# Two merged instructions in a hat step, and a newly derived order of steps, in a convolution and attention kernel

## The chip, the cores and the metric

One Trainium2 chip, one of its cores. The metric is the device time of one launch in microseconds (us); a kernel's time is the median of its runs. The engines are PE (TensorE), DVE (VectorE), ACT (ScalarE), POOL (GpSimd) and SP (SyncE, which here only issues DMAs).

## The reference

Eight images of 56 x 56 places with 128 channels, in float32. Layer 0 is a deformable convolution and an MLP; layer 1 is additive attention and a mixture of 64 experts. Cut to what matters here:

```
xp = x @ w_in + b_in
h  = gelu(bn(depthwise_conv3x3(x)))
offset, mask = h @ w_off + b_off, softmax(h @ w_msk + b_msk)      # 4 groups x 9 taps
y  = bilinear_sample(pad(xp), offset) weighted by mask, summed over the taps, @ w_out
x  = x + gamma1 * layer_norm(y)
x  = x + gamma2 * layer_norm(gelu(x @ w_fc1) @ w_fc2)
# attention over the 3136 tokens t of an image
e  = exp(w2 . tanh(f[i] + g[j] + b1)) for j < i;  t = t + (e @ t) / sum(e)
# experts: per expert the 8 tokens with the highest softmax (over tokens) logits
pooled = sum of 8 tokens by their probability;  out = gelu(pooled @ w1) @ w2
t = t + scatter(out * probability)
```

## The kernel before

**Tiling.** An image is cut into 49 tiles of 64 places (the halves of the 128 partitions hold two pairs of groups), 25 blocks of 128 tokens (the last has 64) and 7 bands of 8 rows. A step is named by what it does and its number: sample 29 works on tile 29, keys 14 on block 14, offsets 6 on band 6.

**The samples.** For a tile, POOL issues an indirect gather for each of up to 18 columns (2 groups x 9 taps, line 1380). It gathers only 16 or 17 of them: the last one or two columns, the "near" ones, are made by PE from a map of the image in SBUF. For two such columns, DVE makes rows of a hat function (step rows, lines 1575 to 1592: how far row and column lie from the sample, clipped and turned to 1 - distance, then spread over four spans of the width), PE turns them (hat), DVE copies them (hat, line 1596), PE multiplies them with the map (near, line 2068), and DVE weighs and sums (near, lines 1602 and 1607). DVE weighs the gathered corners (weigh, line 1620, six instructions) and sums a tile (sample, line 1629). The gathered tiles lie in four slots of pool_mem; tile t may be gathered once the sample of the tile that had its slot is done (tile 4 waits for sample 0, tile 5 for sample 1, tile 33 for sample 29). From tile FULL on, the last image gathers all 18 columns; FULL comes out of the plan and is 4.

**A block's chain.** Two tiles give a block: turn, mix (layer norm, line 1463), turn_mid, hidden (PE, then ACT's gelu), mlp_out, norm, turn_norm, keys (line 1673). Then ACT runs the tanh units of the block (line 1938), whose number and width grow with the block's number; PE sums them (score, line 2128); ACT takes the exp (line 1948); PE turns and multiplies (values), with DVE's copy (line 1697) between; finish, norm2, route and logits follow. conv, offsets (lines 1504 to 1540) and weights (lines 1542 to 1574) make the indices and weights of a band. The steps image_in, project_in, patches, offsets, hat, near, route, logits and those below share one bank of PSUM, side_ps.

**The late work.** Experts can only be chosen when all of an image's logits exist. In the last image's time, the routes of images 0 and 1, 2 and 3, 4 and 5, and 6 are taken: u_in (SP loads the scores, line 1248), u_max, u_match, u_differ (DVE, lines 1745, 1754, 1759), u_exp, u_mul and the pooling. Then come 16 e_hid and 16 e_out (line 1817) for the experts of these seven images, c_expert (line 1822) and 49 c_mix (lines 2240 and 1828), which add the results to the images. The last image's own experts (l_ steps, from l_max at line 1832 on) stand at the end: 16 loads of 2 MB, four of them ahead.

**What sets the order.** Each engine's instructions stand in a fixed order, written by a planner in the same file. `simulate` runs a list scheduler over the steps with what each needs (`needs`), how long it lasts (`LASTS`, `STRETCH`) and when it is due (`due_times` plus a shift by kind, `SHIFT`; for the last image also `LATE_SHIFT`, `ROUTE_AT`, `EXPERT_GAP`). From its result `first_order` writes image 0, `list_schedule` a period that a loop repeats for images 1 to 6 (two images a turn), beginning at sample 0, and `last_order` the last image with the late work. POOL's order is that of the tiles. The step rows in the period needs for each image 36 of its kind; the launch has 255.

```
    todo += [(images - 1, e, s) for e, s in late]
    return in_order(simulate(need, due_of, todo, [x for x in at if x[3] < 0], stretch={"pool": SAMPLES / (NEAR_AT + .5)}))
```

These two lines (788 and 789) end `last_order`. The functions that the change touches:

Of the kernel before, what the change touches and what calls it, by code (L numbers as in the profile page):

```python
# [7 lines left out]
ALU = mybir.AluOpType  # L8
# [14 lines left out]
SAMPLES = GROUPS // 2 * TAPS  # L23
# [18 lines left out]
NEAR_AT = SAMPLES - NEAR  # L42
# [75 lines left out]
ROUTE_AT = (1.395, 5.421, 6.615, 10.365)  # L118
EXPERT_GAP = 0.2662
# [112 lines left out]
def last_user(t):  # L232
# [20 lines left out]
STRETCH = {'pe': 1.0669, 'act': 1.0220, 'dve': 1.0077}  # L253
# [8 lines left out]
    "keys": 2.361, "mix": 0.781, "conv": 1.814, "image_in": 1.885, "logits": -2.464, "patches": -1.253,  # L262
    "norm2": 3.532, "finish": -0.688, "mask": 0.74, "turn_norm": 0.831, "turn_mid": 0.867, "project_in": -1.682,
    "exp": -2.031, "weigh": 1.456, "unit": -2.536, "offsets": 0.04, "norm": -0.292, "values": 0.03, "score": -0.34,
    "mlp_out": -0.92, "x_in": -0.928, "rows": 2.531, "near": -0.291, "hidden": 0.256, "turn": -1.756,
    "sample": 1.692, "weights": 0.726, "route": -0.475, "hat": 0.361,
# [12 lines left out]
FIRST = ("image_in", "project_in", "patches")  # L279

# [5 lines left out]
    ("dve", "rows"): 2.0, ("pe", "hat"): .9, ("dve", "hat"): .8, ("pe", "near"): 1.3, ("dve", "near"): 1.4,  # L286
# [208 lines left out]
def simulate(need, due, todo, earlier=(), early=(), stretch={}, release=None):  # L495
# [10 lines left out]
    now = 0.0  # L506
# [32 lines left out]
    while True:  # L539
        for e in ready:  # L540
# [26 lines left out]
        now, _, what, e, n, step = event  # L567
        if what == "release":
            add(n, e, step)
            continue  # L570
        if what == "free":
            busy[e] = any(x[2] == "free" and x[3] == e for x in events)
        elif (n, step) in early:
            if e == "dve":
                banks[bank_of[n, step]] = True
        elif step[0] in SIDE and e == SIDE_READER.get(step[0], "dve"):
            side_free = True
# [188 lines left out]
def last_order(schedule, images):  # L766
# [16 lines left out]
    return in_order(simulate(need, due_of, todo, [x for x in at if x[3] < 0], stretch={"pool": SAMPLES / (NEAR_AT + .5)}))  # L783
# [44 lines left out]
def network(nc, io, x2_d, xln2_d, logits_d, patches_d, chosen_d, expert_d, map_d, out, images):  # L828
    with ExitStack() as ctx:
        def sb(name, shape, dt=F32):  # L830
            return ctx.enter_context(nc.sbuf_tensor(name, shape, dt))
# [61 lines left out]
        off_row = sb("off_row", [P, 2, H])  # L893
        off_col = sb("off_col", [P, 2, WINDOW])
# [499 lines left out]
        def _(dve):  # L1394
# [75 lines left out]
            def task(n, odd, name):  # L1470
# [104 lines left out]
                elif what == "rows":  # L1575
# [836 lines left out]
```

How the kernel before makes its waits and increments, by code:

```python
            def task(n, odd, name):  # L1170
                what, i = (*name, 0)[:2]
                b = i % 2
                if what == "image_in":
                    sp.wait_ge(band_turned.sem, band_turned.free(n, i, 2))
                    sp.dma_start(x_band[:, b], io["x"][bass.ds(n * S + i * BAND, BAND), :]
                                 .rearrange("(q p) c -> p q c", p=112)).then_inc(x_band_in[b].sem, 16)
                elif what == "patches":
                    sp.wait_ge(patch_ready.sem, patch_ready.after(n, i))
                    if i < 2 and not (isinstance(n, int) and n == 0):
                        sp.wait_ge(sampled.sem, sampled.after(n - 1, -1))
                    if is_early(n):
                        sp.dma_start(patches_d[0][i * P:i * P + patch_rows(i), :],
                                     early_patch[:patch_rows(i), i % EARLY_BANKS].rearrange("p g c k -> p (g c k)"))\
                            .then_inc(early_out[i % EARLY_BANKS], 16)
                        return
                    sp.dma_start(patches_d[int(odd)][i * P:i * P + patch_rows(i), :],
                                 patch[:patch_rows(i), b].rearrange("p g c k -> p (g c k)")).then_inc(patches_out[b].sem, 16)
                elif what == "map_out":
                    sp.wait_ge(in_copied.sem, in_copied.after(n, NBAND - 1))
                    nc.sync.sem_inc(sp_step, 1)
                    sp.wait_ge(map_in.sem, map_in.after(n - 1, 0))
```

## Time and profile before

| | us |
|---|---|
| median of 3 runs (8794.79 to 8805.16) | 8801.63 |
| profiled execution | 8798.16 |
| its span, first to last instruction | 8796.3 |
| first gather begins | 72.06 |
| last gather ends | 8481.51 |
| busy: PE 6909.1, DVE 6651.2, ACT 6757.9, POOL 6354.8 | |

The granted TensorE clock was 0.918 of full speed on average. Busy time leaves out the drains between DVE's dependent instructions and the issue time between POOL's gathers, so the engines are fuller than their shares say. The last image's gathers begin at 7358.4 us; the loop's images take 1036 to 1046 us each.

### The profile page before, as it was taken

The page shows a single profiled execution, that of the slowest core. Times are in us where ns is not written, and L with a number is a line of the kernel's source. Part 1 is how long each engine was busy: PE and PEld are TensorE (multiplying, and loading weights), DVE is VectorE, ACT ScalarE, POOL GpSimd, SP SyncE. Part 2 cuts the span into 40 slices and gives each one's busy share as a digit, 9 for nine tenths or more (in the row PEclk, how much of TensorE's full clock was granted, in tenths as well). Part 3 has the DMA queues.
Part 4 walks back from the last instruction along what each step waited for, and adds up shares of the span by engine and source line. Part 5 has one row for each costly group of instructions (what it writes and reads, how often), then busy time and mean ns, then how long its engine had stood idle before and what let it go on. Part 6 is the DMA issues. An engine that isn't in the chain of part 4 may idle for free.

```text
span 8796.3 us, 163541 instructions
## 1 busy us (share of the span) xinstructions
PE 6909.1 (79%) x50045; PEld 3461.2 (39%) x50045; DVE 6651.2 (76%) x18037; ACT 6757.9 (77%) x8222; POOL 6354.8 (72%) x6550
## 2 busy tenths in 40 slices
PE   5678878788777888778887788878887787767787
PEld 2333433434333333334334343343433333434444
DVE  6778877888778877788777887788877887776553
ACT  1358977788877888788977888768887788878992
POOL 4777777777777777777777777777777777777740
PEclk8789989899999999999998999989999999988997
DMA  3222222222222222222222222222222223335545
GB/s 90 61 79 74 61 61 61 81 70 61 63 68 78 65 63 61 72 80 60 63 60 79 75 62 61 61 83 67 62 63 69 78 64 70 106 101 168 143 125 183
DMA packets 554156, 693.05 MB, mean 79 GB/s; under 512 B 254400, under 2 KB 368960, under 8 KB 551136
## 3 DMA queue, kind: packets, MB, share of 16 engines
q0 software_dynamic: 209472, 429.42, 18.7%
q1 hardware_dynamic: 343808, 252.97, 10.2%
q8 instruction: 426, 6.98, 0.3%
q14 instruction: 450, 3.69, 0.1%
HBM read 568.99 MB, written 112.84 MB: 78 GB/s over the span
## 4 chain that ended last, share of the span: by engine, by line
POOL 38%; DVE 20%; issue 18%; PE 8%; ACT 7%; DVEq 7%; DMA 2%; SPq 0%; POOLq 0%; ACTq 0%
POOL pool_mem L1380 38%; DVEq L1399 6%; ACT tanh L1938 6%; DVE pool_mem L1620 3%; PE side_ps L2068 2%; PE score_ps L2128 2%; DVE y L1629 2%; DVE pool_mem L1607 1%; DVE hat L1602 1%; DVE bst L1446 1%; DVE expoT L1697 1%; DVE near_one L1438 1%; DVE pool_mem L1501 1%; PE side_ps L2038 1%; DVE hat L1589 1%
## 5 line engine op out<-in xcount | busy, mean ns | idle before, releaser
L1938 ACT ACTIVATE tanh<-key_rep,query 128x896 f32<-128x896 f32 (+7 forms) x6400 | 5539.3, 951 | 1131.2 <-DVEq L1399 582.0
L1380 POOL DMA_INDIRECT pool_mem<-patches_odd,pool_mem x3306 | 3214.0, 972 | 1034.3 <-issue 1002.6
L1380 POOL DMA_INDIRECT pool_mem<-patches_even,pool_mem x3240 | 3140.6, 969 | 1092.2 <-issue 978.2
L2128 PE MATMUL score_ps<-tanh,score_w 128*32 128x512 f32 (+3 forms) x24320 | 2680.0, 549 | 383.5 <-ACT tanh L1938 378.4
L2128 PEld LDWEIGHTS score_ps<-tanh,score_w 128*32 128x32 f32 x24320 | 692.4, 113 | 1803.0 <-issue 1140.4
L1620 DVE TENSOR_TENSOR pool_mem<-pool_mem 128x384 f32<-128x384 f32 (+2 forms) x2352 | 1070.2, 524 | 217.1 <-DMA pool_mem<-patches_even,pool_mem 107.5
L2068 PE MATMUL side_ps<-near_map,hatT 112*64 112x480 f32 x4080 | 1051.3, 638 | 202.0 <-DVEq L1399 180.8
L1629 DVE TENSOR_REDUCE y<-pool_mem 128x64 f32<-128x2304 f32 x392 | 999.0, 2548 | 30.8 <-issue 9.9
L2157 PE MATMUL value_ps<-values,expoT 128*128 128x129 f32 (+1 forms) x5200 | 784.9, 292 | 59.4 <-DVE expoT L1697 54.0
L2157 PEld LDWEIGHTS value_ps<-values,expoT 128*128 128x128 f32 (+1 forms) x5200 | 685.4, 199 | 174.3 <-DVE expoT L1697 105.4
L1697 DVE COPY expoT<-turn_ps 128x512 f32<-128x512 f32 (+4 forms) x800 | 456.1, 571 | 172.7 <-issue 100.7
L2007 PE MATMUL turn_ps<-ident,expo 128*128 128x128 f32 (+1 forms) x2632 | 465.0, 292 | 112.9 <-DVE expoT L1697 49.8
L2068 PEld LDWEIGHTS side_ps<-near_map,hatT 112*64 112x64 f32 x4080 | 294.7, 148 | 654.0 <-issue 636.0
L1948 ACT ACTIVATE expo<-score_ps,tiny 128x896 f32<-128x896 f32 (+9 forms) x416 | 382.9, 920 | 156.8 <-PE score_ps L2128 151.2
L1602 DVE TENSOR_TENSOR hat<-side_ps,off_col 128x480 f32<-128x480 f32 x510 | 333.2, 653 | 164.2 <-PE side_ps L2068 137.7
L2007 PEld LDWEIGHTS turn_ps<-ident,expo 128*128 128x128 f32 (+1 forms) x2632 | 313.4, 149 | 314.9 <-issue 149.8
L2038 PE MATMUL side_ps<-pool_mem,early 128*128 128x448 f32 x1008 | 408.2, 560 | 32.9 <-DVEq L1399 32.8
L1607 DVE TENSOR_REDUCE pool_mem<-hat 128x32 f32<-128x480 f32 x510 | 333.8, 655 | 60.9 <-issue 1.4
L1948 ACT ACT_TABLE_LOAD x196 | 251.5, 1283 | 138.1 <-PE score_ps L2128 134.6
L1923 ACT ACTIVATE hid<-chain_ps,b_hid 128x128 f32<-128x128 f32 (+1 forms) x800 | 227.0, 366 | 111.2 <-PE chain_ps L2097 109.4
L2007 PE MATMUL side_ps<-ident,hat 128*112 128x128 f32 x1020 | 191.9, 304 | 151.1 <-DVEq L1399 142.6
L2104 PE MATMUL chain_ps<-w_fc,hid 128*128 128x128 f32 (+1 forms) x1600 | 236.9, 293 | 80.1 <-ACT hid L1923 79.5
(192 smaller groups left out, 7394.9 us busy)
## 6 DMA issues: line engine op xcount, KB each, us to landing
pool_mem<-in_weight SPq DMA_DIRECT2D x64, 1024.0 KB, 9.1
pool_mem<-patches_odd,pool_mem POOLq DMA_INDIRECT x3306
pool_mem<-patches_even,pool_mem POOLq DMA_INDIRECT x3240
patches_even<-pool_mem SPq DMA_DIRECT2D x104, 256.0 KB, 2.0
patches_odd<-pool_mem SPq DMA_DIRECT2D x104, 256.0 KB
pool_mem<-in_x SPq DMA_DIRECT2D x56, 224.0 KB
x_tok<-in_x SPq DMA_DIRECT2D x192, 64.0 KB
x_d<-x SPq DMA_DIRECT2D x192, 64.0 KB
```

What stands on the lines that cost most here:

```text
L1380: pool.indirect_dma_start(gathered[:, b, j * 4 * CG:(j + 1) * 4 * CG], None, patches_flat[int(odd)], bass.IndirectOffsetOnAxis(ap=index[:, ...
L1399: return v.drain()
L1620: v.tensor_tensor(part, part, weight[:, lo:hi].unsqueeze(2) .to_broadcast([P, hi - lo, CG, 4]), ALU.mult)
L1629: v.tensor_reduce(y[:, i // 2 % 2, b].rearrange("p (g c) -> p g c", c=CG), product.rearrange("p (g t) c k -> p g c t k", g=2), AX_XY, ALU. ...
L1697: last = v.tensor_copy(expoT[:rows_, pi % 2, z[0]:z[1], :r], turn_ps[:rows_, z[0]:z[1], :r])
L1938: nc.scalar.activation(tanh[:, TANH_AT[ui][0]:TANH_AT[ui][1]], key_rep[:, lo:lo + w], ACT.Tanh, bias=query[:, col:col + 1]).then_inc(tanh_ ...
L1948: nc.scalar.activation(expo[:r, ci % 2, :w], score_ps[:r, ci % 2, :w], ACT.Exp, bias=tiny[:r, 2:3])\
L2007: return mm(out, src, ident[:r, :r], is_transpose=True, start=True, stop=True)
L2038: last = mm(side_ps[:, :BAND], taps[:, t], x_pad[:, i * BAND_ROWS + dy:(i + 1) * BAND_ROWS + dy, dx:dx + W], start=t == 0, stop=t == TAPS - 1)
L2068: last = mm(side_ps[h * SUB:(h + 1) * SUB, :CG * WINDOW], hatT[:HALF_ROWS, b, part, h * SUB:(h + 1) * SUB], near_map[:HALF_ROWS, h, part], ...
L2128: last = mm(score_ps[32 * col:32 * col + 32, ci % 2, lo:hi], score_w[:, place], tanh[:, TANH_AT[ui][0] + lo:TANH_AT[ui][0] + hi], start=pl ...
L2157: last = mm(value_ps[:r, :C + 1], expoT[:wj, pi % 2, z, :r], values[:wj, value_place(odd, j)], start=j == 0, stop=j == k)
```

## The change

The rows and columns of the hat lie in one tile, `off`, of 56 + 15 values for each of two samples. The subtractions stay two instructions; the mirror (negative distance) and the clip are now one each over both. The step has five instructions, not seven. The planner is changed with it: rows lasts 1.75, not 2.0, the side bank is free for PE's next step as soon as DVE has read it in near and offsets (0.8 and 0.85 after the begin), the gather time of the last image is given tile by tile, and the numbers that shift the steps are others. FULL is 6, not 4, so that the last image's tiles 4 and 5 gather 17 and 16 columns and three near columns more are made; there are 257 rows steps.

```diff
-ROUTE_AT = (1.395, 5.421, 6.615, 10.365)
-EXPERT_GAP = 0.2662
+ROUTE_AT = (0.665, 1.92, 5.635, 7.017)
+EXPERT_GAP = 0.1326
...
-STRETCH = {'pe': 1.0669, 'act': 1.0220, 'dve': 1.0077}
+STRETCH = {'pe': 1.0560, 'act': 1.0116, 'dve': 0.9975}
...
-    "sample": 1.692, "weights": 0.726, "route": -0.475, "hat": 0.361,
+    "sample": 4.156, "score": -0.806, "turn": -1.86, "turn_mid": 0.602, "turn_norm": 0.831, "unit": -1.662,
...
+SIDE_READ = {"near": .8, "offsets": .85}
...
-    ("dve", "rows"): 2.0, ("pe", "hat"): .9, ("dve", "hat"): .8, ("pe", "near"): 1.3, ("dve", "near"): 1.4,
+    ("dve", "rows"): 1.75, ("pe", "hat"): .9, ("dve", "hat"): .8, ("pe", "near"): 1.3, ("dve", "near"): 1.4,
...
+        if step[0] in SIDE_READ and engine == "dve" and at + SIDE_READ[step[0]] > 0:
+            events.append((at + SIDE_READ[step[0]], serial, "side", engine, n, step))
+            serial += 1
...
+            if e == "pool" and whole is not None and n == whole[0] and step[1] >= whole[1]:
+                end = now + SAMPLES * GATHER_US
...
-        off_row = sb("off_row", [P, 2, H])
-        off_col = sb("off_col", [P, 2, WINDOW])
+        off = sb("off", [P, 2, H + WINDOW])
+        off_row, off_col = off[:, :, :H], off[:, :, H:]
...
-                    v.scalar_tensor_tensor(off_row[:, :m], off_row[:, :m], -1.0, off_row[:, :m], ALU.mult, ALU.min)
-                    v.scalar_tensor_tensor(off_col[:, :m], off_col[:, :m], -1.0, off_col[:, :m], ALU.mult, ALU.min)
-                    settle()
-                    v.tensor_scalar(off_row[:, :m], off_row[:, :m], -1.0, 1.0, ALU.max, ALU.add)
-                    v.tensor_scalar(off_col[:, :m], off_col[:, :m], -1.0, 1.0, ALU.max, ALU.add)
+                    v.scalar_tensor_tensor(off[:, :m], off[:, :m], -1.0, off[:, :m], ALU.mult, ALU.min)
+                    settle()
+                    v.tensor_scalar(off[:, :m], off[:, :m], -1.0, 1.0, ALU.max, ALU.add)
                     settle()
```

Three places show how the steps move. The changed file has up to nine lines more, so that L2068 becomes L2075, L2007 becomes L2014, L1629 becomes L1636.

**The end of the loop's period, PE.** Before, from turn 24 (chain_ps from y) to near 4 (side_ps from near_map), the last PE step of the period:

```order
L2080 MATMUL chain_ps<-ident,y 64x64 x4
L1983 REGISTER_ALU
L2128 MATMUL score_ps<-tanh,score_w 32x512 x4
L2128 MATMUL score_ps<-tanh,score_w 32x384 x4
L1983 REGISTER_ALU
L2128 MATMUL score_ps<-tanh,score_w 32x512 x4
L2128 MATMUL score_ps<-tanh,score_w 32x384 x4
L1983 REGISTER_ALU
L2007 MATMUL turn_ps<-ident,expo 128x128 x4
L1990 REGISTER_ALU
L2068 MATMUL side_ps<-near_map,hatT 64x480 x4
```

After, from turn_norm 23 over keys 23 and near 5 to turn 24 (near 4 stands just ahead of the piece):

```order
L2014 MATMUL chain_ps<-ident,values 128x128
L1990 REGISTER_ALU
L2135 MATMUL score_ps<-tanh,score_w 32x512 x4
L2135 MATMUL score_ps<-tanh,score_w 32x384 x4
L2120 MATMUL chain_ps<-chainT,w_key 128x128
L2121 MATMUL chain_ps<-chainT,w_q 128x128
L1997 REGISTER_ALU
L2075 MATMUL side_ps<-near_map,hatT 64x480 x4
L1990 REGISTER_ALU
L2014 MATMUL turn_ps<-ident,expo 128x128 x4
L1990 REGISTER_ALU
L2087 MATMUL chain_ps<-ident,y 64x64 x4
```

Near 4 and near 5 have moved from behind turn 24 to ahead of it. On DVE, mlp_out 23, norm 23 and offsets 6 have moved the other way past weigh 2, from behind it to ahead of it, and rows 3 stands ahead of sample 0.

**The last image's first route, DVE.** MAX is u_max 0, y is a sample. Before, samples 0 to 2 are done (the last two are shown) and weights 6, mlp_out 24 and norm 24 lie between them and MAX:

```order
L1629 TENSOR_REDUCE y<-pool_mem 128x64
L1648 COPY chainT<-chain_ps 128x64
L1629 TENSOR_REDUCE y<-pool_mem 128x64
...
L1660 TENSOR_SCALAR values<-x,mv,root 64x128
L1697 COPY expoT<-turn_ps 128x512
L1745 MAX early<-pool_mem 128x8
L1747 TENSOR_SCALAR early<-early 128x1
```

After:

```order
L1655 COPY chainT<-chain_ps 128x64
L1752 MAX early<-pool_mem 128x8
L1754 TENSOR_SCALAR early<-early 128x1
L1761 MATCH_REPLACE pool_mem<-early,pool_mem 128x3136
L1766 TENSOR_TENSOR pool_mem<-pool_mem 128x448 x7
L1472 TENSOR_TENSOR ln_a<-chain_ps,rows 64x128
...
L1627 TENSOR_TENSOR pool_mem<-pool_mem 128x128
L1673 COPY chainT<-chain_ps 128x64
L1704 COPY expoT<-turn_ps 128x512
L1636 TENSOR_REDUCE y<-pool_mem 128x64
```

The three steps of the route, then mlp_out 24, norm 24 and weigh 3, stand ahead of sample 0; weights 6, mix 24 and turn_mid 24 are what stands before MAX in the last image's part.

**The end, DVE.** L1828 is a c_mix, MAX is l_max, the row with x7 holds the seven l_turn. Before:

```order
L1733 TENSOR_SCALAR logit<-side_ps,gate_b 64x64
L1832 MAX early<-tanh 64x8
L1834 TENSOR_SCALAR early<-early 64x1
L1835 MATCH_REPLACE tanh<-early,tanh 64x3136
L1837 TENSOR_TENSOR tanh<-tanh 64x3136
L1828 TENSOR_TENSOR pool_mem<-pool_mem,side_ps 112x512 x2
L1841 RECIPROCAL early<-early 64x1
L1843 SCALAR_TENSOR_TENSOR tanh<-tanh,early 64x3136
L1828 TENSOR_TENSOR pool_mem<-pool_mem,side_ps 112x512
L1847 COPY tanh<-score_ps 112x256 x7
```

After:

```order
L1740 TENSOR_SCALAR logit<-side_ps,gate_b 64x64
L1839 MAX early<-tanh 64x8
L1841 TENSOR_SCALAR early<-early 64x1
L1842 MATCH_REPLACE tanh<-early,tanh 64x3136
L1844 TENSOR_TENSOR tanh<-tanh 64x3136
L1848 RECIPROCAL early<-early 64x1
L1850 SCALAR_TENSOR_TENSOR tanh<-tanh,early 64x3136
L1854 COPY tanh<-score_ps 112x256 x7
```

The c_mix are gone from this place: 39 of 49 stood ahead of l_max before, all 49 do now. Their first stands behind keys 14, not keys 17; e_hid begins behind keys 9, not 11, and e_out behind keys 12, not 14.

## Rows read from the trace of the kernel before

**Rows 1.** The page: the chain that ended last, and POOL's two groups.
```profile
POOL 38%; DVE 20%; issue 18%; PE 8%; ACT 7%; DVEq 7%; DMA 2%; SPq 0%; POOLq 0%; ACTq 0%
L1380 POOL DMA_INDIRECT pool_mem<-patches_odd,pool_mem x3306 | 3214.0, 972 | 1034.3 <-issue 1002.6
L1380 POOL DMA_INDIRECT pool_mem<-patches_even,pool_mem x3240 | 3140.6, 969 | 1092.2 <-issue 978.2
```

**Rows 2.** Waits, POOL, whole span: us in total, times, longest.
```profile
POOL pool_mem L1380 <- DVE y L1629: 74.1, 45, 13.7
```

**Rows 3.** Waits, POOL, from 1118 to 7358 us (images 1 to 6).
```profile
POOL pool_mem L1380 <- DVE y L1629: 55.9, 42, 8.3
```

**Rows 4.** Timeline, POOL: start us, us, [idle before]; image 0 tile 5, image 7 tile 4.
```profile
191.06 0.94 POOL L1380 DMA_INDIRECT pool_mem<-patches_even,pool_mem  x1 [13.68 <-DVE y L1629]
...
7446.07 0.94 POOL L1380 DMA_INDIRECT pool_mem<-patches_odd,pool_mem  x1 [4.23 <-DVE y L1629]
```

**Rows 5.** Window 8300:8600 (PE, PEld, DVE, ACT, POOL busy), and ACT's waits in 8582:8641.
```profile
8300.00:8600.00 300.00, 254.84 (x1854) 142.86 (x1850) 148.18 (x383) 294.02 (x320) 138.24 (x143) 0.95 0.41 118
...
ACT expo L1948 <- PE score_ps L2128: 6.7, 2, 6.4
```

**Rows 6.** Timeline, DVE: a near, a copy and a rows step in image 5.
```profile
5324.24 0.65 DVE L1602 TENSOR_TENSOR hat<-side_ps,off_col 128x480 f32<-128x480 f32 x1
...
5326.01 0.27 DVE L1578 TENSOR_TENSOR off_row<-near_y,ruler 128x112 f32<-128x112 f32 x1
...
5327.04 0.18 DVE L1587 TENSOR_SCALAR off_col<-off_col 128x30 f32<-128x30 f32 x1
...
5328.12 0.16 DVE L1707 TENSOR_SCALAR den<-value_ps 128x1 f32<-128x1 f32 x1 [0.21 <-issue]
```

**Rows 7.** Timeline, POOL: the gather over the end of that rows step.
```profile
5326.58 0.96 POOL L1380 DMA_INDIRECT pool_mem<-patches_odd,pool_mem  x1 [0.30 <-issue]
```

**Rows 8.** Timeline, DVE, image 7: weigh 2, mlp_out 23, turn_norm 23, offsets 6, turn 24, sample 0.
```profile
7423.22 2.80 DVE L1620 TENSOR_TENSOR pool_mem<-pool_mem 128x384 f32<-128x384 f32 x6 [8.02 <-DMA pool_mem<-patches_odd,pool_mem]
...
7426.99 0.29 DVE L1463 TENSOR_TENSOR ln_a<-chain_ps,rows 128x128 f32<-128x128 f32 x1
...
7434.79 0.29 DVE L1666 COPY chainT<-chain_ps 128x128 f32<-128x128 f32 x1 [0.48 <-PE chain_ps L2007]
...
7436.94 0.42 DVE L1509 TENSOR_TENSOR pool_mem<-side_ps,grid 128x252 f32<-128x252 f32 x1
...
7441.61 0.29 DVE L1635 COPY chainT<-chain_ps 128x128 f32<-128x128 f32 x1 [0.26 <-issue]
...
7442.75 2.54 DVE L1629 TENSOR_REDUCE y<-pool_mem 128x64 f32<-128x2304 f32 x1
```

**Rows 9.** Timelines, DVE and SP, image 7: weights 6, the route's first load, u_max, u_match, u_differ.
```profile
7458.97 0.28 DVE L1544 TENSOR_REDUCE pool_mem<-pool_mem 128x14 f32<-128x126 f32 x1
...
7462.76 0.39 SPq L1239 DMA_DIRECT2D early<-in_weight  x1
...
7475.79 3.43 DVE L1745 MAX8 early<-pool_mem 128x8 f32<-128x3136 f32 x1 [7.17 <-DMA pool_mem<-logits_d]
...
7480.08 3.41 DVE L1754 MATCH_REPLACE8 pool_mem<-early,pool_mem 128x3136 f32<-128x3136 f32 x1
...
7486.06 3.84 DVE L1759 TENSOR_TENSOR pool_mem<-pool_mem 128x448 f32<-128x448 f32 x7
```

**Rows 10.** The line of e_out (ns min/median/max, first and last start), and c_expert in the timeline.
```profile
L1817 DVE COPY pool_mem<-side_ps x16: 280/292/292, 8123.6 to 8230.1; 128x128 f32<-128x128 f32 x16
...
8238.39 1.23 DVE L1822 TENSOR_TENSOR pool_mem<-pool_mem,early 128x1024 f32<-128x1024 f32 x1 [6.76 <-DMA pool_mem<-expert_d]
```

**Rows 11.** c_mix from 8640 us on and DVE's waits for it; window 8697:8771 of the loads.
```profile
L1828 DVE TENSOR_TENSOR pool_mem<-pool_mem,side_ps x14: 672/688/689, 8641.0 to 8777.7; 112x512 f32<-112x512 f32 x14
...
  DVE pool_mem L1828: 17.8, 11
...
8697.00:8771.00 74.00, 46.65 (x588) 25.45 (x580) 16.07 (x41) 2.80 (x13) 0.00 (x0) 0.79 0.97 348
```

More of the change, by code:

```diff
@@ L261 @@
 LATE_SHIFT = {
[L262 to L265, printed above, removed]
-    "sample": 1.692, "weights": 0.726, "route": -0.475, "hat": 0.361,
+    "conv": 0.912, "exp": -2.106, "finish": -0.559, "hat": -0.168, "hidden": 0.967, "image_in": 1.885, "keys": 2.361,
+    "logits": -2.464, "map_in": 0.428, "mask": -0.934, "mix": 0.781, "mlp_out": -0.92, "near": 1.076, "norm": -0.246,
+    "norm2": 2.196, "offsets": -2.031, "patches": -0.849, "project_in": -1.682, "route": -0.475, "rows": 2.283,
+    "sample": 4.156, "score": -0.806, "turn": -1.86, "turn_mid": 0.602, "turn_norm": 0.831, "unit": -1.662,
+    "values": 2.049, "weigh": 1.456, "weights": 1.186, "x_in": -0.514,
 }
@@ L492, in needs, with simulate @@
     return out
-def simulate(need, due, todo, earlier=(), early=(), stretch={}, release=None):
+def simulate(need, due, todo, earlier=(), early=(), stretch={}, release=None, whole=None):
     waiting, users = {}, {}
@@ L567, in simulate @@
         now, _, what, e, n, step = event
+        if what == "side":
+            side_free = True
+            continue
         if what == "release":
@@ L575, in simulate @@
                 banks[bank_of[n, step]] = True
-        elif step[0] in SIDE and e == SIDE_READER.get(step[0], "dve"):
+        elif step[0] in SIDE and step[0] not in SIDE_READ and e == SIDE_READER.get(step[0], "dve"):
             side_free = True
@@ L782, in last_order @@
     todo += [(images - 1, e, s) for e, s in late]
-    return in_order(simulate(need, due_of, todo, [x for x in at if x[3] < 0], stretch={"pool": SAMPLES / (NEAR_AT + .5)}))
+    return in_order(simulate(need, due_of, todo, [x for x in at if x[3] < 0], whole=(images - 1, full)))
 def units_of(images):
```

## The prediction

> **What bounds the kernel now.** I read the page first, then the waits of POOL, then the timelines around them. The page says that POOL issues 3306 + 3240 = 6546 gathers of 0.97 us each, and that the chain of waits lies on POOL and on "issue" for 56% of the span, on DVE for 20% [rows 1]. The busy share (72%) hides that POOL is full: between two gathers lie 0.30 us of issue, so a gather costs about 1.275 us, and the only other idle time after the first one is 74.1 us in 45 waits for y, that is for the step sample to free a slot [rows 2]. Each of the 45 contains the ordinary 0.30 us, so 60.6 us are real. Of these the loop's six images hold 55.9 - 42 x 0.30 = 43.3 us [rows 3], image 0 holds 13.68 - 0.30 = 13.4 us at tile 5, and the last image 4.23 - 0.30 = 3.9 us at tile 4 [rows 4]. What follows the last gather (the table above has its end), some 315 us, is bound first by ACT, busy for 294.0 of 300 us before 8600 us [rows 5], and then by the expert loads. ACT is fed by the tiles: in the last image its tanh units wait for the keys of their block until block 17, and from then on it never runs dry. A shift of the gathers up to block 17 therefore moves the end by as much.
>
> **The step rows.** It loses two of seven instructions, 0.18 us each in the 1.90 us from 5326.01 to 5327.91 [rows 6]. Over the 257 steps that is at most 257 x 0.36 = 93 us of DVE time and likelier a third of that, since the two that stay read 142 columns instead of 112. None of it counts: POOL is not waiting for it, and DVE's own idle gaps before weigh (8.02 us in the place shown further down) take it up. If this cover were gone, 36 steps an image at 0.13 us would be 5 us an image. The gather that ran while L1587 did took 0.96 us beside its usual 0.94 [rows 7]; 0.02 us for each of 255 steps would be 5 us, and I count none. Beside that row stands a rule of the Trainium skill (SBUF — State Buffer, Who interferes with whom): a VectorE instruction that uses both ports locks GpSimd out of the shared pair until it ends, and then GpSimd can write no DMA descriptors. By that rule a removed TENSOR_SCALAR of this kind gives its whole length back to POOL; that is a rival below, since here the row shows a tenth of it.
>
> **The loop's order.** Before, sample 0 of the next image (which frees the slot of tile 4) stands behind weigh 2, hat 2, mlp_out 23, norm 23, offsets 6 and more: 19.5 us from the start of weigh 2, itself held by its gather, to the start of sample 0 [rows 8]. The new order has mlp_out 23, norm 23 and offsets 6 ahead of weigh 2, and puts near 4, near 5 and rows 3 behind it. What is left behind weigh 2: weigh 2 itself 2.80 + 0.14, turn_norm and keys 7436.94 - 7434.31 = 2.6, turn 24 and a copy 7442.75 - 7441.35 = 1.4 [rows 8], two nears at 1.6 and a rows at 1.8 [rows 6]; together 11.9 us. Sample 0 would begin at 7423.2 + 11.9 = 7435.1 and end at 7437.7; POOL comes to tile 4 at 7446.07 - 4.23 + 0.30 = 7442.1 [rows 4]. That leaves 4.4 us to spare where it lacked 4 to 8. The loop's other tight place is sample 29, which frees the slot of tile 33 (the rest of the 43.3 us). It stood behind weigh 31; now weigh 29 is the last ahead of it, two tiles or some 33 gathers (42 us) earlier. I take 43.3 us as gone but for 3 us of chance waits; bounds: all gone, or 15 us left.
>
> **The first image.** Sample 1 stood behind weigh 4, held by its gather. It now stands behind weigh 3, whose gather lands 17 x 1.275 = 21.7 us earlier: it ends near 191.06 - 21.7 = 169.4, and tile 5 is reached at 191.06 - 13.4 = 177.7 [rows 4]. The wait of 13.4 us goes; the way to the first gather is unchanged.
>
> **The last image.** Here the change adds a wait. The route of images 0 and 1 begins with loads that SP may issue only after weights 6; u_max began 7475.79 - 7462.76 = 13.0 us later and DVE stood 7.17 us for it, but behind sample 0 [rows 9]. The new order puts u_max, u_match and u_differ ahead of sample 0. From the end of the shortened stretch, at the image's start + 76 us, it goes: hat 3 and weights 6 (7462.76 - 7458.97 = 3.8) to 81, the loads to 94, u_max 3.6, u_match 3.6, u_differ 4.0 [rows 9], then mlp_out 24 and norm 24 (5 us: for block 23 the stretch from 7426.99 to 7434.31 holds them and four copies [rows 8]), weigh 3 at 2.9, sample 0 at 2.5 with copies around them: 117. POOL reaches tile 4 at 84. It waits 33 us instead of 3.9: 29.1 us given back. Queued behind are image 6's copies for PE and, through PE, ACT; both have room before block 17. Bounds: 10 us if the loads land early, 45 if PE is late too. Three gathers fewer (the full tiles start at 6, not 4) give 3 x 1.275 = 3.8 us.
>
> **The end.** The experts' steps come two to four blocks earlier. The 16 e_out took 106.5 us and c_expert stood 6.76 us for its load, just as ACT entered its full stretch [rows 10]; now they fall on blocks 12 to 14. There they delay keys 14 by up to 20 us, of which ACT can recover about 14 before block 17, and the stall at block 17 is gone; I take these as even, bounds -5 and +15. All 49 c_mix now stand before l_max; before, 14 of them ran after 8641 us, and DVE waited 17.8 us for them [rows 11]. Ten lie between ACT's last exp and the first new load, and with their 0.69 us each they held that chain by up to 18 us; I take 12, since some waits were covered by ACT and PE. During the loads DMA is at 0.97 with or without them [rows 11], so there only 4.5 us more. PE is relieved of 4 or 5 c_mix after keys 24, where ACT's last exp waited 6.4 us for it [rows 5]: 4 us. The end gives 20.5; bounds 0 and 33.
>
> **The sum:** -13.4 - 43.3 + 3 + 29.1 - 3.8 + 0 - 20.5 = -48.9 us. Against the profiled execution's 8798.16 us, which is 3.5 us under the median, this is 8749.3 us.
>
> **Rivals.**
> 1. *Slower: the loop's sample 0 comes late after all.* Near 4, near 5 and rows 3 now stand before it, each through the one side bank of PE, which has scores of its own between them. The mechanism costs six times its wait. It cancels the 48.9 at 8 us an image and makes the kernel slower by 0.2% at 11, so sample 0 would have to come 15.6 us later than I count. For it: DVE waits for L1602 occur. Against: in this place turn_norm waited only 0.48 us for PE [rows 8]. At 13 us an image: -48.9 - 3 + 78 = +26, 8824 us.
> 2. *The end gives nothing and keys 14 stays late.* The expert loads bound the end with or without c_mix, and the packed e_out cost 15 us at block 17: -48.9 + 20.5 + 15 = -13.4, 8785 us. For it: DMA at 0.97 in the loads. Against: ten c_mix lie ahead of them.
> 3. *The last image does not stall.* If the route's load is there when DVE comes, the 29.1 us stay: 8720 us. For it: DVE is often held elsewhere; against: 13.0 us of load follow weights 6 in any order.
> 4. *The port.* If every TENSOR_SCALAR removed gave its 0.18 us back to POOL, 255 x 0.18 = 46 us more: 8703 us. Against it, the 0.96 beside 0.94 us. This is the Trainium skill's lock, named above.
> 5. *The change does nothing where it counts:* the plan moves steps but DVE waits for the same gathers, and only the end differs: -13.4 - 3.8 - 4 = -21, 8777 us.
>
> **How the numbers follow.** My case 0.66, rival 5 0.05, rival 3 0.08, rival 4 0.02, rival 2 0.12, rival 1 0.07. The range 8720 to 8786 takes in rivals 2, 3 and 5; outside lie rivals 1 and 4 and the tails of my case, together under 0.2. Against the median 8801.63 a difference of 0.2% is 17.6 us, about what a measurement can tell from no change. My case and rivals 3, 4 and 5 are faster by more: 0.81. Rival 2 and my case's slow edge: 0.12. Slower by more than 0.2%: 0.07.
>
> **What would show it.** Right: POOL's waits for y fall from 74.1 us to some 35 to 45 and are nearly all one wait in the last image at tile 4; no wait at tile 5 of image 0; DVE stands about 9 us before the first MAX8, which comes ahead of the image's first y; no row of L1828 (c_mix) behind the last MAX8; ACT's last exp near 8607, the last gather near 8453. Wrong: waits of 3 us or more at tile 4 in the loop's images (rival 1), or MAX8 for image 7 following ACT's last exp as late as before, 14 us (rival 2).

## The result and the profile after

The changed kernel takes 8750.5 us (median of 3 runs, 8747.33 to 8752.43) against 8801.63: a ratio of 0.9943, 95% interval 0.9920 to 0.9965. The forecast was 8749.3. From one profiled execution to the other (8798.16 to 8752.43) the change is 45.7 us, where 48.9 were forecast.

The page of the changed kernel, its span, busy times, the chain that ended last and POOL's two groups, beside [rows 1]:

```profile
span 8750.6 us, 163133 instructions
...
PE 6894.0 (79%) x50077; PEld 3450.2 (39%) x50077; DVE 6621.8 (76%) x17545; ACT 6769.0 (77%) x8236; POOL 6352.6 (73%) x6547
...
POOL 50%; issue 19%; DVE 12%; ACT 7%; PE 6%; DVEq 4%; DMA 2%; SPq 1%; POOLq 0%; ACTq 0%
...
L1389 POOL DMA_INDIRECT pool_mem<-patches_odd,pool_mem x3303 | 3208.3, 971 | 1042.5 <-issue 1004.0
L1389 POOL DMA_INDIRECT pool_mem<-patches_even,pool_mem x3240 | 3144.1, 970 | 1058.6 <-issue 983.4
```

The gathers are as long as before, and DVE is busy for 29.4 us less, of which little or nothing was waited for in this kernel (e2, e8 below). What has gone is waiting: POOL and its issue are now 69% of the chain, before 56%, DVE 12%, before 20%. POOL's waits for y over the whole span (us in total, times, longest), then the same from 1103 to 7303 us, the loop's six images, which answer to [rows 2] and [rows 3]:

```profile
POOL pool_mem L1389 <- DVE y L1636: 42.2, 21, 36.1
...
POOL pool_mem L1389 <- DVE y L1636: 5.5, 18, 0.3
```

In the loop the longest is 0.3 us, the ordinary issue time: none of 42 waits is left. POOL's timeline at tile 5 of image 0 and at tile 4 of image 7, beside [rows 4] (start us, us, [idle before]):

```profile
178.91 0.94 POOL L1389 DMA_INDIRECT pool_mem<-patches_even,pool_mem  x1 [0.30 <-issue]
...
7422.66 0.94 POOL L1389 DMA_INDIRECT pool_mem<-patches_odd,pool_mem  x1 [36.07 <-DVE y L1636]
```

The first wait is gone; the second has grown from 4.23 to 36.07 us and is nearly all that is left of the 42.2. What holds it: the route's first load on SP (image 7 begins at 7302.7 us),

```profile
7384.88 0.42 SPq L1248 DMA_DIRECT2D early<-in_weight  x1
```

and then DVE's timeline, from the last copy ahead of u_max to weigh 3 and sample 0:

```profile
7388.38 0.23 DVE L1655 COPY chainT<-chain_ps 128x64 f32<-128x64 f32 x1
7399.38 3.43 DVE L1752 MAX8 early<-pool_mem 128x8 f32<-128x3136 f32 x1 [10.77 <-DMA pool_mem<-logits_d]
...
7415.84 2.62 DVE L1627 TENSOR_TENSOR pool_mem<-pool_mem 128x384 f32<-128x384 f32 x6
...
7419.33 2.54 DVE L1636 TENSOR_REDUCE y<-pool_mem 128x64 f32<-128x2304 f32 x1
```

The loads begin 82.2 us into the image, MAX8 (u_max) comes 14.5 us later, and sample 0 starts 116.6 us into the image. At the other end, ACT's last exp with its wait for PE, beside [rows 5]:

```profile
8605.41 0.95 ACT L1955 ACTIVATE expo<-score_ps,tiny 64x832 f32<-64x832 f32 x1 [3.58 <-PE score_ps L2135]
```

Then the lines of c_mix and of l_max with first and last start, beside [rows 11]; no c_mix is left behind l_max:

```profile
L1835 DVE TENSOR_TENSOR pool_mem<-pool_mem,side_ps x49: 674/686/690, 8078.4 to 8552.7; 112x512 f32<-112x512 f32 x49
...
L1839 DVE MAX8 early<-tanh x1: 3420/3420/3420, 8617.1 to 8617.1; 64x8 f32<-64x3136 f32 x1
```

The same marks in both kernels give a ledger that adds up to the two spans (us, each rounded by itself, so that a row can be off by 0.1; POOL's last gather ends, ACT's last exp begins, l_max begins, the span ends):

| | last gather | to last exp | to l_max | to the end | span |
|---|---|---|---|---|---|
| before | 8481.5 | 157.7 | 14.8 | 142.4 | 8796.3 |
| after | 8453.9 | 151.5 | 11.7 | 133.5 | 8750.6 |
| difference | -27.6 | -6.2 | -3.1 | -8.8 | -45.7 |

### The profile page after: what moved, and what is told of

The parts are those of the page before. It is cut to its first block, busy times and chain, and to the rows that moved or that the text cites. A ratio compares the mean times of both kernels' runs of the same rounds, so it can differ in the third digit from the quotient of the medians.

```text
span 8750.6 us, 163133 instructions
## 1 busy us (share of the span) xinstructions
PE 6894.0 (79%) x50077; PEld 3450.2 (39%) x50077; DVE 6621.8 (76%) x17545; ACT 6769.0 (77%) x8236; POOL 6352.6 (73%) x6547
## 3 DMA queue, kind: packets, MB, share of 16 engines
q1 hardware_dynamic: 343808, 252.97, 10.2%
## 4 chain that ended last, share of the span: by engine, by line
POOL 50%; issue 19%; DVE 12%; ACT 7%; PE 6%; DVEq 4%; DMA 2%; SPq 1%; POOLq 0%; ACTq 0%
POOL pool_mem L1389 50%; ACT tanh L1945 6%; DVEq L1408 3%; DVE pool_mem L1627 2%; DVE y L1636 2%; PE score_ps L2135 1%; PE side_ps L2075 1%; DVE pool_mem L1614 1%; PE value_ps L2164 1%; DVE hat L1609 1%; DMA expert_d<-pool_mem 0%; DVE hat L1596 0%; DMA pool_mem<-in_weight 0%; DVE bst L1455 0%; PE side_ps L2045 0%
## 5 line engine op out<-in xcount | busy, mean ns | idle before, releaser
L2075 PE MATMUL side_ps<-near_map,hatT 112*64 112x480 f32 x4104 | 1022.2, 620 | 209.8 <-DVEq L1408 208.1
L1636 DVE TENSOR_REDUCE y<-pool_mem 128x64 f32<-128x2304 f32 x392 | 997.8, 2547 | 20.8 <-issue 6.6
L2014 PE MATMUL turn_ps<-ident,expo 128*128 128x128 f32 (+1 forms) x2632 | 470.8, 293 | 101.6 <-DVE expoT L1704 38.0
L2075 PEld LDWEIGHTS side_ps<-near_map,hatT 112*64 112x64 f32 x4104 | 288.7, 144 | 663.6 <-issue 647.7
L2014 PEld LDWEIGHTS turn_ps<-ident,expo 128*128 128x128 f32 (+1 forms) x2632 | 316.5, 150 | 293.8 <-issue 168.3
L1609 DVE TENSOR_TENSOR hat<-side_ps,off 128x480 f32<-128x480 f32 x513 | 334.7, 652 | 120.3 <-PE side_ps L2075 96.2
L2014 PE MATMUL side_ps<-ident,hat 128*112 128x128 f32 x1028 | 203.6, 317 | 175.0 <-DVEq L1408 170.6
L2104 PE MATMUL chain_ps<-chainT,w_fc 128*128 128x128 f32 (+1 forms) x1600 | 247.6, 302 | 113.8 <-DVE chainT L1655 113.4
```

Source lines behind the costliest of these rows:

```text
L1609: v.tensor_tensor(part, side_ps[:, :CG * WINDOW].rearrange("p (c x) -> p c x", x=WINDOW), off_col[:, i % 2:i % 2 + 1, :].to_broadcast([P, ...
L1636: v.tensor_reduce(y[:, i // 2 % 2, b].rearrange("p (g c) -> p g c", c=CG), product.rearrange("p (g t) c k -> p g c t k", g=2), AX_XY, ALU. ...
L2014: return mm(out, src, ident[:r, :r], is_transpose=True, start=True, stop=True)
L2075: last = mm(side_ps[h * SUB:(h + 1) * SUB, :CG * WINDOW], hatT[:HALF_ROWS, b, part, h * SUB:(h + 1) * SUB], near_map[:HALF_ROWS, h, part], ...
```

## The experiments

The changed kernel was timed beside the kernel before on its own; the others were timed in four sessions (e1 to e4, e5 to e8, e9 to e11, e12) beside it, so the table gives ratios to before of the same session. The median of before was 8801.63 us in the first of these sessions and 8794.3 to 8798.47 in the four others, so medians of different sessions compare to within some 7 us only. The ledger's columns come from each kernel's profile.

| kernel | us (runs) | ratio, 95% interval | waits for y | last gather | to last exp | to l_max | to the end | span |
|---|---|---|---|---|---|---|---|---|
| after | 8750.5 (3) | 0.9943, 0.9920 to 0.9965 | 42.2 | 8453.9 | 151.5 | 11.7 | 133.5 | 8750.6 |
| e1 | 8788.83 (11) | 0.9991, 0.9982 to 1.0000 | 61.0 | 8469.4 | 160.3 | 14.8 | 145.2 | 8789.6 |
| e2 | 8755.51 (5) | 0.9951, 0.9937 to 0.9964 | 35.7 | 8456.5 | 153.1 | 12.0 | 133.3 | 8754.9 |
| e3 | 8723.73 (5) | 0.9916, 0.9902 to 0.9929 | 7.9 | 8418.0 | 161.0 | 11.6 | 136.9 | 8727.5 |
| e4 | 8784.34 (10) | 0.9993, 0.9977 to 1.0009 | 65.9 | 8482.5 | 149.2 | 11.7 | 133.9 | 8777.3 |
| e5 | 8738.19 (5) | 0.9936, 0.9922 to 0.9949 | 7.9 | 8415.2 | 158.3 | 15.8 | 142.4 | 8731.7 |
| e6 | 8763.99 (5) | 0.9964, 0.9951 to 0.9978 | 40.1 | 8442.0 | 151.9 | 17.5 | 142.4 | 8753.8 |
| e7 | 8757.85 (5) | 0.9960, 0.9946 to 0.9973 | 54.3 | 8458.9 | 151.3 | 11.7 | 133.9 | 8755.8 |
| e8 | 8747.36 (5) | 0.9946, 0.9933 to 0.9960 | 38.8 | 8446.8 | 153.3 | 11.6 | 134.2 | 8746.0 |
| e9 | 8738.85 (5) | 0.9937, 0.9924 to 0.9951 | 7.0 | 8418.7 | 172.5 | 11.2 | 135.8 | 8738.2 |
| e10 | 8727.60 (5) | 0.9925, 0.9912 to 0.9939 | 4.9 | 8414.7 | 156.9 | 19.8 | 135.5 | 8726.9 |
| e11 | 8810.39 (11) | 1.0021, 1.0012 to 1.0030 | 73.2 | 8479.8 | 178.5 | 15.3 | 134.4 | 8808.1 |
| e12 | 8728.87 (5) | 0.9920, 0.9907 to 0.9934 | 9.5 | 8417.3 | 159.4 | 15.4 | 135.3 | 8727.4 |

Waits for y of 5 to 8 us in total are the ordinary issue times alone.

### e1: the merged step alone

The kernel before with the five instructions and nothing of the planner.

```diff
-                    v.scalar_tensor_tensor(off_row[:, :m], off_row[:, :m], -1.0, off_row[:, :m], ALU.mult, ALU.min)
-                    v.scalar_tensor_tensor(off_col[:, :m], off_col[:, :m], -1.0, off_col[:, :m], ALU.mult, ALU.min)
+                    v.scalar_tensor_tensor(off[:, :m], off[:, :m], -1.0, off[:, :m], ALU.mult, ALU.min)
                     settle()
-                    v.tensor_scalar(off_row[:, :m], off_row[:, :m], -1.0, 1.0, ALU.max, ALU.add)
-                    v.tensor_scalar(off_col[:, :m], off_col[:, :m], -1.0, 1.0, ALU.max, ALU.add)
+                    v.tensor_scalar(off[:, :m], off[:, :m], -1.0, 1.0, ALU.max, ALU.add)
```

> The kernel before with the merged rows step alone (five instructions), the planner and so the order of steps as before. My theory (only the order counts, POOL is the path): 8800 us, within 5 us of before, with POOL's waits for y at 70 to 75 us in 45 times and DVE's busy time some 35 us less. Rival (the DVE time that the merge saves is what was gained): 8750 to 8770 us.

POOL's waits for y in it, beside [rows 2]:

```profile
POOL pool_mem L1380 <- DVE y L1627: 61.0, 40, 13.7
```

It gives 6.6 us (8788.83 against 8795.42), and the interval of its ratio reaches 1.0000, so this is at the edge of the noise. The waits shrink by 13.1 us, 11.3 us of it real waits in the loop (43.3 to 32.0); the 13.4 us in image 0 stay. I had expected them to stay at 70 to 75 us, and that was wrong. The last gather ends 12.1 us sooner and the span shrinks by 6.7, since the end is 5.4 us worse. So the step is worth something where samples are late: about a seventh of the 45.7 us, and far from the rival's 8750 to 8770 us.

### e2: the order alone

The changed kernel with the seven instructions (the diff of e1 the other way round).

> The changed kernel with the rows step's mirror and clip as four instructions again (seven in all), its order of steps kept. My theory: 8750 us, at most 5 us more, since DVE's 0.13 us a step does not reach POOL; POOL's only long wait stays the one of 33 to 37 us at tile 4 of the last image. Rival (the merge is the gain): 8780 to 8800 us.

It has no wait for y but the one of 33 us and lies 4.3 us above the changed kernel's span; the two ratios overlap. The new order carries the gain.

### e3: sample 0 ahead of the route

```diff
-    "sample": 4.156,
+    "sample": 2.5,
```

> The changed kernel with the last image's shift of sample at 2.5 instead of 4.156, so that sample 0 and samples 1 and 2 stand ahead of u_max 0. My theory (the last image's wait of 35.8 us at tile 4 is all given back at the end, since ACT from block 17 on follows POOL): the wait falls under 5 us and the time to 8719 us, between 8710 and 8730. Rival (the end is bound by ACT's total work or by PE, so the wait was hidden): 8745 to 8750 us.

POOL waits for y nowhere:

```profile
POOL pool_mem L1389 <- DVE y L1636: 7.9, 26, 0.3
```

The last gather comes 35.9 us sooner than in the changed kernel, the end 23.1 us sooner: 9.5 us are lost again on the way to the last exp and 3.4 behind it. At 8723.73 us this is the fastest of all. It was not timed beside the changed kernel: the intervals of the two ratios, 0.9902 to 0.9929 and 0.9920 to 0.9965, still touch, and it is the ledger that says where the 23.1 us come from.

### e4, e7 and e8: more and less DVE time in the step, and the port

e4 issues the mirror three times, e7 the clip three times (the first two with `+ 0.0`), e8 leaves the mirror out, so that its near columns are weighted otherwise.

```diff
+                    v.tensor_scalar(off[:, :m], off[:, :m], -1.0, 0.0, ALU.max, ALU.add)
+                    settle()
+                    v.tensor_scalar(off[:, :m], off[:, :m], -1.0, 0.0, ALU.max, ALU.add)
+                    settle()
                     v.tensor_scalar(off[:, :m], off[:, :m], -1.0, 1.0, ALU.max, ALU.add)
```

> The changed kernel with the mirror instruction issued three times (the second and third change nothing), order kept: 257 steps longer by two instructions of about 0.31 us and their drains, some 0.78 us each, 200 us of DVE time. My theory: DVE's slack takes nearly all of it; one rows step stands between weigh 2 and sample 0, so sample 0 comes 0.8 us later and has 4 to spare: 8750 to 8760 us. Rival (DVE is as full as POOL): over 8850 us.

> The changed kernel with the clip (TENSOR_SCALAR over off, 0.24 us) issued three times in each rows step, 2 x 257 = 514 more. Rival 4 (each TENSOR_SCALAR holds POOL's descriptors for its whole length): 514 x 0.24 = 121 us more on POOL, the images grow by 15 us each, about 8870 us. Theory (a gather under it takes 0.02 us longer and no more, what the longer mirror of the other run cost came by DVE's time alone): the gathers' busy time grows by at most 10 us, the images by 2 to 5 us each, 8770 to 8785 us, the same within 8 us per us of DVE time as with the mirror issued three times (8784).

> The changed kernel without the mirror (SCALAR_TENSOR_TENSOR over off): the hat's negative side is left unmirrored, so the near columns are weighted wrongly; four instructions in a rows step. It takes a further 257 x 0.38 = 98 us off DVE. Theory (DVE has slack once no wait for y is left, and the fifth to the seventh instruction cost 4 us between them): 0 to -5 us against the changed kernel, 8745 to 8751 us. Rival (the 34 us for 200 us of added DVE time are a rate that holds in both directions): -17 us, 8733 us.

The three clips of one step in e7, from DVE's timeline in image 5:

```profile
5251.30 0.23 DVE L1594 TENSOR_SCALAR off<-off 128x142 f32<-128x142 f32 x1
5251.61 0.24 DVE L1596 TENSOR_SCALAR off<-off 128x142 f32<-128x142 f32 x1
5251.93 0.24 DVE L1598 TENSOR_SCALAR off<-off 128x142 f32<-128x142 f32 x1
```

The gather that runs over them, from POOL's, and two gathers that run over the next weigh, with that weigh from DVE's:

```profile
5251.43 0.94 POOL L1389 DMA_INDIRECT pool_mem<-patches_odd,pool_mem  x1 [0.30 <-issue]
...
5259.05 1.26 POOL L1389 DMA_INDIRECT pool_mem<-patches_odd,pool_mem  x1 [0.30 <-issue]
5260.62 1.10 POOL L1389 DMA_INDIRECT pool_mem<-patches_odd,pool_mem  x1 [0.30 <-issue]
...
5258.95 2.76 DVE L1631 TENSOR_TENSOR pool_mem<-pool_mem 128x384 f32<-128x384 f32 x6
```

POOL's two groups on e7's page:

```profile
L1389 POOL DMA_INDIRECT pool_mem<-patches_odd,pool_mem x3303 | 3202.9, 970 | 1046.0 <-issue 1005.0
L1389 POOL DMA_INDIRECT pool_mem<-patches_even,pool_mem x3240 | 3143.4, 970 | 1066.1 <-issue 982.0
```

The gather lies over the end of the first clip and all of the second and third, and takes the usual 0.94 us. In total the gathers are busy for 6346.3 us, 6.1 less than in the changed kernel, with 514 clips more; profiles with the same loop differ by up to 9.5 us (6344.0 in e6 to 6353.5 in e9). The 316 gathers of e7 that a clip overlaps by 0.15 us or more last 0.956 us in the mean, the 6143 that none touches 0.971. That comparison is not a fair one, since gathers under a weigh or under the last instruction of a rows step are longer (see the last section). Without those, it is 0.960 us under a clip (194 gathers) and 0.949 under none (4919). So a clip of 0.26 us costs a gather about 0.01 us. Rival 4 is dead for this instruction: 514 clips that held POOL for their whole length would have cost over 120 us, and the span grew by 5.2. The clip is a quick kind, 0.175 us for 30 values and 0.236 for 142 (medians), where the mirror takes 0.183 and 0.307; whether it uses both ports for that no trace shows. In [rows 7], the 0.96 us beside 0.94 cannot be put down to L1587 either: the step's last instruction, L1589, began 0.25 us before that gather ended.

What the added time costs is waiting, and not in proportion; e7 came out below even my own range, e4 far above its own. e7 adds some 180 us of DVE time (137 busy, the rest between instructions) and its span grows by 5.2 us; e4 adds some 200 and grows by 26.7. In e4 the waits return at tile 43 of five of the loop's images (2.4 to 4.9 us each), in e7 only twice, by 0.6 and 1.2 us, with 1.0 us or less at three other tiles of the loop and 5.1 us at tile 46 of image 0. So e7 stands near the point where the slack at that sample runs out. e4's last gather ends 23.6 us after e7's: real waits of POOL make 11.3 of them and longer gathers 11.7; 10.7 of these lie on gathers that a weigh or the last instruction of a rows step overlaps. Whether the added mirrors bring that about was not shown. e4's runs scatter too (8765.9 to 8848.05). e8 takes 98 us off DVE and its ratio is that of the changed kernel: as expected, below the fifth instruction nothing that these intervals can tell is to be had.

### e5: the last image's numbers of before

```diff
-ROUTE_AT = (0.665, 1.92, 5.635, 7.017)
-EXPERT_GAP = 0.1326
+ROUTE_AT = (1.395, 5.421, 6.615, 10.365)
+EXPERT_GAP = 0.2662
```

LATE_SHIFT, too, is that of the kernel before.

> The changed kernel with the last image's numbers (LATE_SHIFT, ROUTE_AT, EXPERT_GAP) of the kernel before; the loop's period and FULL = 6 stay. Theory (my ledger: the loop's waits carry the gain, the last image's new wait and the better end nearly cancel, +29.1 against -20.5): POOL's waits for y fall below 12 us, no 30 us wait in image 7, some 14 c_mix behind l_max again as before; -13.4 - 43.3 + 3 - 3.8 = -57.5 against before, some 8738 to 8750 us, so within 8 us of the changed kernel or up to 12 us below it. Rival (the gain sits in the last image's order): the time goes back towards before, 8775 us or more.

8738.19 us, in the range. Its last gather ends 66.3 us sooner than before's; my terms for it, 13.4 + 43.3 + 3.9 + 3.8, are 64.4. And behind the last gather its three distances are those of before within 1 us (158.3, 15.8, 142.4 against 157.7, 14.8, 142.4). So the period, image 0 and FULL are worth 66 us here and the old last part nothing more. It also follows that the new numbers of the last image, taken together, brought no gain: with the old ones the ratio is 0.9936, with the new ones 0.9943, and the profiled span is 18.9 us shorter with the old. Their better end does not pay for the wait of 36 us that they add.

### e6: fourteen c_mix held behind the last exp

```diff
             put(when + .05 * q, "pe", ("c_mix", n, q), at("sp", "c_in", n), at("dve", "c_expert"),
+                *([at("act", "exp", *list(CHUNK_INDEX)[-1])] if j >= 35 else []))
```

> The changed kernel, but the c_mix of the last two images (14 of 49) may not start on PE before ACT's last exp, so 9 of them stand behind l_max and 5 between the last exp and l_max. Theory (c_mix in the last chain costs what I took for the end, 12 + 4.5 + 4 us): the image and its waits for y stay (42 us), and the time from the last exp to the end grows by 12 to 20 us: 8762 to 8771 us. Rival 2 (the expert loads bound the end with or without c_mix): at most 4 us, 8750 to 8755 us.

The c_mix from 8605 us on, in e6's groups by form:

```profile
L1836 DVE TENSOR_TENSOR pool_mem<-pool_mem,side_ps 112x512 f32<-112x512 f32 x11 | 7.5, 686 | 13.5 <-PE side_ps L2248 13.1 <-issue 0.4
```

Its last exp, from ACT's timeline:

```profile
8593.86 0.95 ACT L1956 ACTIVATE expo<-score_ps,tiny 64x832 f32<-64x832 f32 x1 [3.58 <-PE score_ps L2136]
```

From the last exp to the end it takes 159.9 us, the changed kernel 145.2: c_mix at the end cost 14.7 us, 5.8 ahead of l_max and 8.9 behind it. The profiled span is only 3.2 us longer, since this run's last gather ended 12.0 us sooner (its gathers are busy for 8.4 us less). The median, 8763.99, is in the range too. Yet last gather to last exp is 151.9 as in the changed kernel, and the last exp waits 3.58 us for PE, not 6.45 as before. That part is not c_mix's doing.

### e9, e10, e11 and e12: where the experts stand

e11 is the kernel before with the changed ROUTE_AT and EXPERT_GAP alone. e9 is the changed kernel with LATE_SHIFT of before and ROUTE_AT (1.395, 3.0, 5.0, 7.0). e10 and e12 are e3 with ROUTE_AT (2.0, 4.0, 6.0, 8.0) and EXPERT_GAP 0.2, and with ROUTE_AT (1.5, 3.5, 5.635, 7.5).

```diff
-ROUTE_AT = (1.395, 5.421, 6.615, 10.365)
-EXPERT_GAP = 0.2662
+ROUTE_AT = (0.665, 1.92, 5.635, 7.017)
+EXPERT_GAP = 0.1326
```

> The kernel before with ROUTE_AT and EXPERT_GAP of the changed one and nothing else: seven instructions, the old period, FULL = 4. Theory (the end gives 15 us by c_mix and 7 us by PE, and the early experts cost 0 to 12 us before block 18): POOL's waits for y stay at 65 to 75 us, no c_mix behind l_max, -10 to -22 us against before, 8773 to 8785 us. Rival 2 of the prediction (the end gives nothing): 8790 us or more.

> The changed kernel with LATE_SHIFT of before (no wait of 33 us in image 7) and ROUTE_AT = (1.395, 3.0, 5.0, 7.0), EXPERT_GAP as changed, so that all c_mix stand ahead of l_max. Theory (the two gains add: 66 us of gathers as with the last part of before, and 15 us of c_mix plus 7 us of PE in the last blocks, less what the early experts cost before block 18): at least 14 and at most 27 us below the 8738 of that run less 12 for the experts' delay: 8715 to 8726 us. Rival (the early experts' delay is DVE's and takes the whole end gain back): 8735 us or more.

> The changed kernel with sample 2.5, as in the run that had sample 0 first, and the routes and experts spread (ROUTE_AT = (2.0, 4.0, 6.0, 8.0), EXPERT_GAP = 0.2). In that run the units of block 18 began 62.4 us after their last gather, against 50.2 us where the routes and experts came late. Theory (the packed late work on DVE and PE costs those 12 us): the distance falls to 52 to 58 us, and the time is 8712 to 8722 us. Rival (the distance has another cause, such as sample 0's place): 60 us or more, 8724 us or above.

> The changed kernel with sample 2.5 and ROUTE_AT = (1.5, 3.5, 5.635, 7.5), EXPERT_GAP as changed: between the run with sample 0 first (units of block 18 begun 62.4 us after their gather; last exp to l_max 15.2 us) and the run with the experts apart (55.8 us; 24.6 us, with c_mix in between). Theory (what the experts' place gives before block 18 it takes again between the last exp and l_max, as c_mix end later): distance 55 to 60 us, last exp to l_max 16 to 22 us, 8718 to 8726 us, no more than 6 us from the 8723.7 us of the first of the two. Rival (the two costs can be had apart): 8716 us or less.

e11 falls outside what I expected: 15 us slower than before, not 10 to 22 faster. The end does give what it should (134.4 us from l_max on, not 142.4). But from the last gather to the last exp it takes 178.5 us, 20.9 more than before. Its line of e_out:

```profile
L1817 DVE COPY pool_mem<-side_ps x16: 290/291/292, 8026.8 to 8099.7; 128x128 f32<-128x128 f32 x16
```

DVE's timeline at c_expert and keys 14 (L1673):

```profile
8107.55 1.23 DVE L1822 TENSOR_TENSOR pool_mem<-pool_mem,early 128x1024 f32<-128x1024 f32 x1 [4.02 <-DMA pool_mem<-expert_d]
...
8110.40 0.29 DVE L1673 COPY key_rep<-chain_ps 128x128 f32<-128x128 f32 x1 [0.20 <-issue]
```

ACT behind keys 14:

```profile
8111.38 4.77 ACT L1938 ACTIVATE tanh<-key_rep,query 128x896 f32<-128x896 f32 x5 [17.13 <-DVEq L1399]
```

The 16 e_out come in 73 us instead of 106.5 [rows 10] and stand, with c_expert's wait for its load, ahead of keys 14; ACT is dry for 17.1 us there. The units of block 18 begin 67.0 us after the block's last gather, before 50.9 (by the single records). That is the price that rival 2 named for the packed e_out, 15 us.

e9 pays it as well: 172.5 us to the last exp, and its 8738.85 us is e5's time, though the end is better. That is the rival of its expectation, and my theory of an added gain falls. In e3, with the new LATE_SHIFT, the same place costs less, 161.0. e10 spreads the experts; the distance to the last exp falls to 156.9 and block 18 stands at 55.9 us, as expected, but five c_mix come between the last exp and l_max (19.8 us, not 11.6), and the time, 8727.60, is above the range I gave. e12, in between, has block 18 at 59.5 us, 159.4 and 15.4 in the table (its expectation counts the second from the begin of the last exp's wait; so counted it is 20.2), and 8728.87 us, 3 us above my range and far from the rival's 8716. The two costs trade against each other as the last image is planned here; neither beats e3.

Of the last exp's wait for PE: it is 6.45 us in before, e1, e5, e9 and e11, the kernels with the old LATE_SHIFT, and 3.57 to 4.81 us in those with the new one, whether c_mix stand late (e6) or early. The whole stretch from the first unit of block 18 to the last exp shows the same split: 359.7 to 362.8 us with the old one, ACT idle for 15.5 to 19.3 of them, and 349.0 to 352.2 us with the new one, ACT idle for 7.1 to 10.2. Which of its entries does that was not tried.

## Why the prediction was right

The time was met to 1.2 us, which is closer than the three runs agree with each other (5.1 us), and most steps hold on their own.

- **The image 0 wait** (-13.4): gone. Tile 5 starts at 178.91 us; I had it reached at 177.7.
- **The loop** (-43.3 + 3): all gone, no residue. The order of steps does it, not the shorter step (e2, e5). "None of it counts" of the step holds for the changed kernel (e8, e2) and not for the kernel before, where it gave 6.6 us (e1): there samples were late, so DVE time ahead of them was POOL time.
- **The last image's wait** (+29.1, "It waits 33 us instead of 3.9"): 35.8 instead of 3.9, so +31.8. The chain was right link by link: loads from 82.2 us (81), MAX8 at 96.7 (94), sample 0 done at 119.2 (117).
- **The last gather:** 27.6 us sooner, the sum of my terms was 28.4. It ends at 8453.9 us (8453), the last exp begins at 8605.4 (8607), and DVE stands 10.8 us before u_max (9).
- **"I take these as even, bounds -5 and +15", and 4 us of PE relief:** together -6.2 us measured, where -4 was forecast. The delay came much as said: block 14's units begin 56.9 us after the block's last gather, before 39.9, and at block 18 only 2.5 us of these 17.0 are left (53.4, before 50.9). But the reason that I gave, that ACT recovers them by itself, holds only beside POOL's wait: where that wait is gone, block 18 stands at 62.5 us (e3), and the early experts cost 15 us and more in e9 and e11 (20.9). That DVE gains on the gathers during the wait is my reading of this and was not tried by itself. What makes up for it comes behind block 18, where the stretch to the last exp is 10.3 us shorter (349.4 against 359.7), and this goes with the new LATE_SHIFT and not with the c_mix that I put the 4 us down to (e6, e11). My "it never runs dry" from block 17 on was too strong: before, ACT was idle for 15.5 us of that stretch. With 1.6 us by which the gathers behind block 18's take less time, the three add up to -6.2.
- **The end** (12 + 4.5 for c_mix): 11.9 between the two kernels, 14.7 where c_mix alone move (e6). I had 12 ahead of the first new load and 4.5 during the loads. That load begins 57.8 us after the last exp in the kernel before, 49.8 in the changed one and 60.6 in e6, and from there to the end it takes 99.3, 95.4 and 99.3 us. So c_mix cost 10.8 and 3.9 us by e6, and the split holds too.
- **The rivals:** 1, late samples in the loop: refuted by the waits of 0.3 us. 4, the port: refuted by e7; the Trainium skill's lock (SBUF — State Buffer, Who interferes with whom) does not show for this TENSOR_SCALAR, which costs a gather about 0.01 us and not its 0.26. 3, no stall in the last image: the route's load was the bound as said, and e3 shows what its absence is worth, 23 us of span and not 29 or 32. 5, a plan that changes only the end: refuted, since none of the loop's 42 waits is left. 2: its first half, an end that gives nothing, is refuted (e6); its second half, keys 14 late, is true of the experts' place by itself and was the rival I had dismissed too lightly. Had the changed kernel had e11's 178.5 us, it would have come out at about 8778.

So part of the hit is luck: two terms whose reasons were wrong as given, the recovery of ACT and PE's relief, stood near their sum.

## What to carry to other kernels

Where a producer (here POOL) waits for a consumer's step (here a sample on DVE) to free a buffer, look at what stands just ahead of it. Steps that could run earlier should stand ahead of the one that is held by the producer's newest work, not between that one and the step that frees the buffer. The new order of image 0 and of the loop, with FULL, gave 66 us up to the last gather; shortening a step of the same engine gave 7. A filler moved off the final chain is not free where it lands: ask what it now stands ahead of and which engine that feeds (here keys 14 for ACT), and try the filler's place by itself. A wait that is added in one place can hide a delay in another, so the terms of a ledger are measured one at a time, and again together.

## What was not expected of the hardware

A gather's busy time is 0.94 us in most records and 0.97 in the mean, and what lies between is not spread evenly. In the changed kernel the 991 gathers that a weigh overlaps by 0.15 us or more last 1.062 us in the mean, and the 262 others that the last instruction of a rows step (L1596) overlaps so 1.044; those that neither touches last 0.950. In the kernel before it is 1.071, 1.037 and 0.949, in e7 1.063, 1.046 and 0.949. Both instructions multiply two tensors that lie in SBUF. The product of near (L1609), which reads one of its two from PSUM, goes with 0.954 (530 gathers). The clip, which reads one tensor, goes with gathers that are about 0.01 us longer (e7). Over a launch the gathers under a weigh or an L1596 are some 140 to 150 us longer than at 0.945 us each, in both kernels alike (147 before, 143 after), so this is no part of the gain. It is read from the overlaps alone: no run here moves or removes a weigh, and the cause is not shown. It does say that DVE time under the gathers is not all alike to POOL.

The sum over the 6543 gathers, of which the loop holds most in the same order, varies between profiles by 9.5 us, 0.15% of it, which limits what a single profile can say of any effect on POOL.
